# One-hot lanes stored side by side and made pair by pair on VectorE, in a routed expert kernel

## The reference

```python
ys = y * scale
d = rsqrt(einsum('bi,io->bo', ys * ys, weight * weight) + EPS)
hidden = einsum('bsi,io->bso', x * ys[:, None, :], weight) * d[:, None, :]

logits = hidden @ wr.T
vals, idx = top_k(logits, 2)                     # gating = softmax over the two
mask = (idx[:, :, None] == arange(E)).any(axis=1)
pos = cumsum(mask, axis=0) - 1
keep = mask & (pos < cap)
dispatch[e, pos] = token where keep              # the list of tokens of each expert
xg = hidden[dispatch]
h = gelu(einsum('ecd,edf->ecf', xg, w1) + b1)
y = einsum('ecf,efd->ecd', h, w2) + b2
out = x + segment_sum(y * gate, dispatch)
```

## Time and profile before

| | us |
|---|---|
| median of 3 runs | 952.57 |
| lowest and highest | 951.37, 953.0 |
| the profiled execution's own time | 954.04 |
| its span, first to last instruction | 952.0 |
| PE busy | 932.3 (98%) |
| PEld busy | 892.4 (94%) |
| ACT busy | 537.6 (56%) |
| DVE busy | 470.6 (49%) |
| POOL busy | 409.4 (43%) |

### The profile page before, as it was taken

How to read it: one execution, slowest core, us unless ns; L and a number is a source line. 1 busy time by engine, 2 the same in 40 slices (tenths; PEclk the granted TensorE clock), 3 DMA queues, 4 the chain that set the end, 5 groups by cost and what they waited for, 6 DMA issues and landing times.

```text
span 952.0 us, 19269 instructions
## 1 busy us (share of the span) xinstructions
PE 932.3 (98%) x6447; PEld 892.4 (94%) x6448; DVE 470.6 (49%) x1084; ACT 537.6 (56%) x1223; POOL 409.4 (43%) x419
## 2 busy tenths in 40 slices
PE   8999999999999999999999999999999999999994
PEld 5666799999999999999999999999999999999994
DVE  4488867546444454346444454455444543443441
ACT  5888554656555565456555655556555555555551
POOL 0000214636545445445445455355355355455443
PEclk9999999999999999999999999999999999999998
DMA  9566293352622342323522353225223223223223
GB/s 332 182 223 224 74 343 66 53 129 52 138 34 52 51 125 50 48 40 51 133 43 47 45 133 48 41 50 134 39 51 45 39 51 47 37 52 50 34 34 33
DMA packets 53559, 82.18 MB, mean 86 GB/s; under 512 B 6736, under 2 KB 42576, under 8 KB 53136
## 3 DMA queue, kind: packets, MB, share of 16 engines
q0 software_dynamic: 26496, 36.76, 24.3%
q1 hardware_dynamic: 25472, 44.44, 13.9%
q10 hardware_dynamic: 1552, 0.53, 0.2%
HBM read 54.17 MB, written 35.93 MB: 95 GB/s over the span
## 4 chain that ended last, share of the span: by engine, by line
PE 96%; DVE 1%; ACT 1%; DMA 1%; issue 0%; POOL 0%; SPq 0%; DVEq 0%; POOLq 0%
PE bank L565 14%; PE bank L566 14%; PE bank L567 14%; PE bank L552 14%; PE bank L553 14%; PE bank L554 13%; PE bank L461 5%; PE bank L542 3%; PE bank L509 2%; PE bank L474 2%; PE bank L476 2%; DMA sb_w<-in_w 1%; ACT sb_hid_t L702 0%; POOL out_rows L386 0%; ACT sb_x L667 0%
## 5 line engine op out<-in xcount | busy, mean ns | idle before, releaser
L734 ACT ACTIVATE sb_h_raw<-bank,sb_b_now 128x384 f32<-128x384 f32 x368 | 215.0, 584 | 282.8 <-PE bank L554 266.3
L1083 DVE TENSOR_TENSOR sb_h_lo<-sb_h_raw,sb_h_hi 128x384 fp32r<-128x384 f32 x368 | 204.9, 557 | 296.4 <-ACT sb_h_hi L734 287.0
L565 PE MATMUL bank<-sb_w_hi,sb_h_hi 128*128 128x256 f32 x1104 | 315.1, 285 | 0.0
L566 PE MATMUL bank<-sb_w_lo,sb_h_hi 128*128 128x256 f32 x1104 | 310.8, 282 | 0.0
L567 PE MATMUL bank<-sb_w_hi,sb_h_lo 128*128 128x256 f32 x1104 | 310.1, 281 | 0.0
L386 POOL DMA_INDIRECT out_rows<-sb_y,sb_add_ids x138 | 233.5, 1692 | 89.9 <-DVE sb_y L1106 54.8
L552 PE MATMUL bank<-sb_xt_hi,sb_w_hi 128*128 128x384 f32 x736 | 249.6, 339 | 0.5 <-ACT sb_h_hi L734 0.5
L554 PE MATMUL bank<-sb_xt_hi,sb_w_lo 128*128 128x384 f32 x736 | 248.8, 338 | 0.0
L553 PE MATMUL bank<-sb_xt_lo,sb_w_hi 128*128 128x384 f32 x736 | 248.8, 338 | 0.0
L734 ACT ACTIVATE sb_h_hi<-bank,sb_b_now 128x384 fp32r<-128x384 f32 x368 | 212.8, 578 | 0.0
L566 PEld LDWEIGHTS bank<-sb_w_lo,sb_h_hi 128*128 128x128 f32 x1104 | 208.2, 189 | 0.0
(11 more groups left out here) (136 smaller groups left out, 597.0 us busy)
## 6 DMA issues: line engine op xcount, KB each, us to landing
sb_w_raw<-in_w SPq DMA_DIRECT2D x16, 1024.0 KB
hidden<-sb_rows SPq DMA_DIRECT2D x4, 2112.0 KB, 9.6
sb_x<-in_x_t SPq DMA_DIRECT2D x16, 512.0 KB, 4.7
out_rows<-in_x SPq DMA_DIRECT2D x16, 512.0 KB, 6.4
sb_xg<-hidden,sb_gather_ids POOLq DMA_INDIRECT x138
out_rows<-sb_y,sb_add_ids POOLq DMA_INDIRECT x138
sb_b<-in_b SPq DMA_DIRECT2D x1, 1024.0 KB, 8.9
hidden<-sb_empty SPq DMA_DIRECT2D x3, 132.0 KB, 8.4
```

Source lines behind the costliest of these rows:

```text
L565: pe.matmul(y, hi, w_hi[u][:, cols], start=(f == 0 and s != 1), stop=False, skip_group_check=True)
L566: pe.matmul(y, hi, w_lo[u][:, cols], start=False, stop=False, skip_group_check=True)
L734: ins = act.activation(h, h_bank[f % H_BANKS][:, 0:SLOTS], ACT.Gelu_apprx_tanh, bias=b1_now[u][:, f:f + 1])
L1083: dve.tensor_tensor(h_lo[f % RING][:, :], h_raw[f % RING], h_hi[f % RING][:, :].bitcast(F32), ALU.subtract).then_inc(h_ready, 1)
```

## The change

A pair tile's lanes now lie side by side: the lane areas have the order (c, j, n) instead of (c, n, j). `list_group` makes each pair tile's lanes by one TENSOR_SCALAR over 128 elements: it compares the lane numbers (`row_sb`, a new constant) with the token's lane (`lane_of`, one fp32 number per partition) and multiplies by the token's number (`ids_sb`, likewise). So there are eight such operations in place of the comparison and the product over 1024 elements, and the semaphore `lanes_ready` goes. They come first, then the comparison of the columns, as before. `lane_of` and `ids_sb` become fp32. The load of `row_sb` (128 × 128 fp16, 32 KB) is the last one that ACT issues, and `CONSTS` is 9.

```diff
-        ids_sb = sb("middle_ids", [P, T // P], F16)
+        ids_sb = sb("middle_ids", [P, T // P])
+        row_sb = sb("lane_row", [P, P], F16)
...
-        lane_of = [sb(f"lane_of{u}", [P, 2, TS], F16) for u in range(2)]
+        lane_of = [sb(f"lane_of{u}", [P, 2, TS]) for u in range(2)]
...
-        def hot_area(tile, i, n):
+        def hot_area(tile, i, n, order="p (c n j) -> p c n j"):
             size = TOP_K * n * TILES
             flat = tile[:, :].bitcast(F16)[:, i * size:(i + 1) * size]
-            return flat.rearrange("p (c n j) -> p c n j", c=TOP_K, j=TILES)
-
-        lane_ring = [hot_area(h_raw_sb, i, P) for i in range(HOT_RING)]
+            return flat.rearrange(order, c=TOP_K, j=TILES)
+
+        lane_ring = [hot_area(h_raw_sb, i, P, "p (c j n) -> p c j n") for i in range(HOT_RING)]
...
-        CONSTS = 8
+        CONSTS = 9
...
-                        mm = pe.matmul(list_part[part], lane_hot(g)[:, c, :, j],
+                        mm = pe.matmul(list_part[part], lane_hot(g)[:, c, j, :],
                                        col_hot(g)[:, c, :, j],
...
+            act.dma_start(row_sb[:, :], lane_row).then_inc(const_in, 16)
...
-            def one_hot(hot, n, of, g):
+            def list_group(g):
 
                 at = g % JOINED * TILES
-                shape = [P, TOP_K, n, TILES]
-                return dve.tensor_tensor(hot, lane_sb[:, 0:n, :].unsqueeze(1).to_broadcast(shape),
-                                         of[g // JOINED % 2][:, :, at:at + TILES].unsqueeze(2).to_broadcast(shape),
-                                         ALU.is_equal)
-
-            def list_group(g):
-
+                u = g // JOINED % 2
                 dve.wait_ge(lanes_found, g // JOINED + 1)
                 if HOT_RING <= g < LAST_SET:
                     dve.wait_ge(listed, g - HOT_RING + 1)
-                hot = lane_hot(g)
-                one_hot(hot, P, lane_of, g).then_inc(lanes_ready, 1)
-                one_hot(col_hot(g), COLS, col_of, g).then_inc(cols_ready, 1)
-                dve.wait_ge(lanes_ready, g + 1)
-                numbers = ids_sb[:, g * TILES:(g + 1) * TILES].unsqueeze(1).unsqueeze(1)
-                dve.tensor_tensor(hot, hot, numbers.to_broadcast([P, TOP_K, P, TILES]),
-                                  ALU.mult).then_inc(lanes_numbered, 1)
+                for c in range(TOP_K):
+                    for j in range(TILES):
+                        tile = g * TILES + j
+                        ins = dve.tensor_scalar(lane_hot(g)[:, c, j, :], row_sb[:, :], lane_of[u][:, c, at + j:at + j + 1],
+                                                ids_sb[:, tile:tile + 1], ALU.is_equal, ALU.mult)
+                ins.then_inc(lanes_numbered, 1)
+                shape = [P, TOP_K, COLS, TILES]
+                dve.tensor_tensor(col_hot(g), lane_sb[:, :, :].unsqueeze(1).to_broadcast(shape),
+                                  col_of[u][:, :, at:at + TILES].unsqueeze(2).to_broadcast(shape),
+                                  ALU.is_equal).then_inc(cols_ready, 1)
```

More of the change, by code:

```diff
@@ L74, with build @@
 assert COLS * P < NO_SLOT and MID <= 1 << 11 and SETS % 2 == 0
-def build(nc, x, x_t, cond_t, w, wr_t, w1, b1_t, w2, b2, ident, tri, expert_low, slot_base, middle_ids, lanes,
+def build(nc, x, x_t, cond_t, w, wr_t, w1, b1_t, w2, b2, ident, tri, expert_low, slot_base, middle_ids, lanes, lane_row,
           early_consts, plan_consts, slot_consts, out):
@@ L196, in lane_hot @@
             at = (g - LAST_SET) % 2 * (TOP_K * P * TILES)
-            return flat[:, at:at + TOP_K * P * TILES].rearrange("p (c n j) -> p c n j", c=TOP_K, j=TILES)
+            return flat[:, at:at + TOP_K * P * TILES].rearrange("p (c j n) -> p c j n", c=TOP_K, j=TILES)
         def col_hot(g):
@@ L243, in build @@
         slots_ready = sem("slots_ready")
-        lanes_ready = sem("lanes_ready")
         cols_ready = sem("cols_ready")
@@ L1173, in constants @@
         "slot_base": np.tile(np.arange(E, dtype=np.float32) * (TILES_E * P) - 1, (P, 1)),
-        "middle_ids": (np.arange(T // P)[None, :] * P % HALF + p[:, None] - MID).astype(np.float16),
+        "middle_ids": (np.arange(T // P)[None, :] * P % HALF + p[:, None] - MID).astype(np.float32),
         "lanes": np.tile(np.repeat(np.arange(COLS), TILES).astype(np.float16), (P, 1)),
+        "lane_row": np.tile(p.astype(np.float16), (P, 1)),
         "early_consts": np.concatenate([block_end, spare_id[:, 0:EARLY_TILES] + NO_SLOT], 1).astype(np.float32),
```

## The result

| | before | changed |
|---|---|---|
| median, us | 951.69 (7 runs, 951.37 to 953.0) | 955.06 (7 runs, 953.5 to 955.74) |
| ratio | | 1.0028, 95% interval 1.0016 to 1.0039 |
| the profiled execution, its span | 954.04, 952.0 | 953.54, 951.5 |
| DVE busy in it | 470.6 | 480.2 |

The kernel became slower, by some 2.7 us going by the ratio (1.5 to 3.7 by its interval). The forecast was no change that a run could show, 952.3, within 949.8 to 955.0; the median, 955.06, lies just outside, on the side where the prediction had put rival C (955.7).

What follows compares the result with a forecast made beforehand. The prediction took TensorE (PE) as the bound: 0.3 us less on PE, 0 for DVE and 0 for the constants, set against the median of 952.57, gave 952.3 us, within 949.8 to 955.0.

Steps and rivals of the forecast that it cites:

- rival C: On DVE, TENSOR_SCALARs with two [P,1] operands come 0.26 us apart, PE idles 3.1 us, 955.7 us; chance 12%.
- the price of the TENSOR_SCALAR: On DVE, 0.13 us from start to start, a group 1.81 us instead of 1.97, 2.6 us gained on DVE.
- the low end: Lower bound for a TENSOR_SCALAR on DVE: 0.12 us start to start, at half of L816's time per element.
- threshold of 176 ns: TENSOR_SCALAR spacing on DVE, 0.21 us more per group, from which a loss starts to show.
- The slack: DVE's lead over PE's ninth matmul: 0.42 us at 58 us, 0.41 at 85; 0.48 at group 12's burst.
- the new order: Lanes made before columns in each group on DVE: changes nothing, since PE waits for both.
- PE would wait for the mask anyway: Burst at 116.0 us, left out of the chain, which goes through ScalarE's copy and DVE's choice of experts.
- The pace of PE: List matmul L509: moving operand sets its pace, spacing stays 152 ns; 0.3 us gained over 112 matmuls.
- A: Rival: the weights set the list matmul's pace; contiguous it falls towards 70 ns, 9.2 us gained, 943.4 us; 6%.
- B: Rival: stepping weight loads only disturb the moving reads; list matmuls at 131 ns, 2.4 us gained, 950.2 us; 10%.
- The forecast of 97 ns for the weight load: L509's weight load on PE falls from 116 to about 97 ns once its weights are contiguous.
- The constants: One more 32 KB DMA and larger token numbers at the start: hidden, 0 us; 0.5 us if the cover were gone.

Runs made afterwards that it cites:

- experiment 4: Kernel before plus sets of eight DVE operations of each form at its start; TENSOR_SCALARs 0.223 us apart with two per-partition operands, 0.163 with one, 0.104 with none.
- experiment 2: Kernel before with the columns (moving operand) contiguous and the lanes left stepping; ratio 0.9932 to before, 6.5 us faster.
- experiment 5: Kernel before plus one unused DVE comparison of 1024 elements in each group, nothing of the change; ratio 1.0096 to before.
- experiment 8: Kernel before with the columns at a step of two fp16 numbers in place of four; 947.71 us, ratio 0.9956 to before.
- experiment 11: Kernel before plus two unused DVE comparisons of 352 elements in each group; ratio 1.0017 to before.
- experiment 9: Changed kernel's eight TENSOR_SCALARs a group, but groups 0, 1, 4, 5 and 12 by two passes with stepping lanes; ratio 1.0014 to the kernel before.
- experiment 12: Eight TENSOR_SCALARs a group only in groups 2, 3, 6, 7, 13, 14 and 15, the others by two passes; ratio 0.9997 to the kernel before.
- experiment 1: Kernel before with the lanes contiguous as in the change, but still made by two passes over 1024 elements; ratio 0.9997 to before.
- experiment 6: Kernel before with lanes and columns both contiguous, made in passes over a whole group; 948.99 us, ratio 0.9969 to before.
- experiment 3: Changed kernel with DVE's split of a weight piece moved behind the two groups of lists in iterations 6 and 10; ratio 1.0014 to the kernel before.
- experiment 7: Kernel before with contiguous columns and all of DVE's weight-piece splits at the end of the iteration; 944.04 us, ratio 0.9913 to before.

## Why the prediction was wrong

**The step that failed is the price of the TENSOR_SCALAR.** The prediction took 0.13 us from start to start, bounds 0.12 to 0.26; it is 0.223 (experiment 4), and the group takes 2.56 us instead of 1.81. It went by L816, which has immediates, as "nearest in form". That row was right for what it is: a form without operands per partition costs 0.104, even less than the 0.13. But this form has two, and L1106, some 60 ns above L816, had shown the price of one. The right reading was in the rows: the low end, 0.12, and L1106's 60 ns twice make 0.24. Rival C had the 60 ns once and made up for it by a rate per element that was too slow.

**Rival C is what happened,** at 12%. Its threshold of 176 ns was passed, and PE waits where it said, with DVE as the releaser: 0.91, 0.89 and 0.26 us. Its price, 0.26, was above the 0.223 measured, and two of its terms were off. The slack was 0.15 us too large: it ran to the start of the ninth matmul, but that starts only 0.15 us after DVE has ended what PE waits for (56.47 against the columns' end at 55.47 + 0.85 = 56.32). With 0.27, 0.26 and 0.33 of slack: 2 × 0.59 − 0.27 = 0.91, 0.92, and 0.59 − 0.33 = 0.26, where 0.91, 0.89 and 0.26 were measured. Part of this is the new order, which the prediction put at nothing ("changes nothing, since PE waits for both"): where the product comes last, as before the change, and PE waits for it, the ninth matmul starts 0.06 us after it (experiments 2, 5, 8 and 11), which puts some 0.09 us of each wait down to the order; no run changes the order alone.

And C left out the mask, which the prediction dismissed in a clause ("PE would wait for the mask anyway"). In the kernel before, PE didn't wait there, though it had nothing to spare. Experiments 9 and 12 show this place: 0.80 us with groups 8 to 11 by single operations, none without.

**The pace of PE was right.** It is all but unchanged, 151 ns for 153, as the byte count of the moving operand had it, and the 0.3 us forecast from it came out at some 0.2; experiments 1 and 2 show it from both sides, 8 the scale. So A and B are out.

**The forecast of 97 ns for the weight load was wrong.** The reading behind it, that the step costs the load 19 ns, was nearly right; what it missed is that stepping columns beside the load cost as much, and that the two don't add up:

```profile
L511 PEld LDWEIGHTS bank<-sb_b,sb_h_raw x96: 110/113/131, 54.2 to 111.4; 128*128 128x128 f16 x96
...
L520 PEld LDWEIGHTS bank<-sb_b,sb_h_raw x96: 95/98/98, 54.5 to 113.0; 128*128 128x128 f16 x96
```

The first line is experiment 2 (stepping weights, contiguous columns), the second experiment 6 (neither steps). Contiguous weights load in 116 ns while stepping columns stream (changed kernel, experiment 1); but the first load of each burst, ahead of which no list matmul runs, takes 95 to 98 ns in the changed kernel and 112 to 117 in the one before. L493's 97 was such a case of neither stepping. The miss had no price, since the load is not what PE waits for.

**The constants were hidden,** as said: DVE's wait for the added one is 0.9 us at the start, and experiment 12, which loads it too, shows no loss. Experiment 5 doesn't load it and has a granted clock of 1.00 up to 40 us; `modulate`'s first matmuls of the third and sixth group start at 19.09 and 35.18 there, at 19.05 and 35.15 in the changed kernel.

Two things stay open. One is the 5.7 us that DVE stood still in experiment 5. It happens at the entry of an expert, other filler code doesn't have it, and the kernel before has 3.4 us at the same places, which would fit the code's place rather than the work; no run shows it. It is not part of the change's loss, since the changed kernel has none. The other is the size of the loss at the mask, 0.46 us in the changed kernel and 0.80 in experiment 9, with the same groups 8 to 11.

## What to carry to other kernels

Price an operation by its operands: many short operations with numbers per partition cost mostly those, so that two passes over 1024 elements (1.20 us) beat eight operations of 128 (1.79), although each of the eight does the work of both passes. When an engine off the critical path gets slower, list every place where another engine takes something from it, with what the handover itself takes (0.06 or 0.15 us here), and follow it through the idle times; repairing one place can open the next (the 0.48 us for the mask in experiment 3). And ask of each matmul which operand sets its pace: here the lanes were made contiguous, and the columns would have brought 6.5 us (8.3 with experiment 7's order).

## What the runs showed of the hardware

- On VectorE each [P,1] operand of a TENSOR_SCALAR costs 60 ns: 104, 163 and 223 ns from start to start with none, one and two (128 fp16 numbers).
- A moving operand of 168 fp16 columns takes 73 ns at a step of one, 77 at two, 152 at four. The Trainium skill (SBUF — State Buffer, section Door 1) says that a step of up to eight 2-byte elements is free; for two the runs nearly agree, for four they don't, at 2.1 times the time.
- A weight load of 128 × 128 fp16 numbers takes 98 ns when neither it nor the moving operand beside it steps, and 113 to 116 when either does.
- A matmul that waits for DVE starts 0.06 us after the end of the operation where that is the lanes' product, 0.15 where it is the columns' comparison.
- One piece of some 3.5 us at the lower clock level (1.2 GHz) cost 1.65 us in the kernel before, and the runs of one kernel on one chip differ by up to 3.3 us (950.96 to 954.27). A difference of 2 us in a span of 950 can't be read from two profiles, but it can from distances inside them.
